# A mixture-of-experts stage on one core: from every expert on every token to visits of 128 scattered rows

## What is computed

```python
h = layernorm(x).reshape(T, d)                 # T = 2048, d = 256
scores = softmax(h @ gate_w.T)                 # 16 experts
topk_w, topk_idx = top_k(scores, 6)
cw = zeros((T, 16)); cw[t, topk_idx[t]] += topk_w[t]
y = 0
for e in range(16):
    g = h @ w_gate[e].T                        # 176 columns
    u = h @ w_up[e].T
    y = y + cw[:, e:e + 1] * (silu(g) * u @ w_down[e].T)
x = x + y
```

## Time and profile before

| | |
|---|---|
| runs, us | 647.69, 657.57, 657.59 (median 657.57) |
| span of the profiled execution, us | 653.6 |
| PE busy | 593.8 us (91%), 3642 matmuls |
| DVE busy | 402.8 us (62%) |
| ACT busy | 295.4 us (45%) |
| POOL busy | 167.2 us (26%) |
| TensorE clock granted, mean | 0.962 |

### The profile page before, as it was taken

How to read it: one execution, slowest core, us unless ns; L and a number is a source line. 1 busy time by engine, 2 the same in 40 slices (tenths; PEclk the granted TensorE clock), 3 DMA queues, 4 the chain that set the end, 5 groups by cost and what they waited for, 6 DMA issues and landing times.

```text
span 653.6 us, 10661 instructions
## 1 busy us (share of the span) xinstructions
PE 593.8 (91%) x3642; PEld 468.5 (72%) x3642; DVE 402.8 (62%) x772; ACT 295.4 (45%) x479; POOL 167.2 (26%) x261
## 2 busy tenths in 40 slices
PE   5889999887888658699999999999999999999995
PEld 4667777663555446588888888888888888888884
DVE  5757877689989635367666555555555555555553
ACT  3585666468879633344444333333333333333331
POOL 6534775938868562000000000000000000000000
PEclk9789999799989857899999999999999999999999
DMA  9700000000000042344543132111231221231211
GB/s 254 254 2 2 1 3 2 1 1 2 1 2 1 1 162 77 87 129 135 141 133 104 59 97 98 65 65 65 64 124 63 64 68 66 82 100 65 64 60 46
DMA packets 37464, 45.90 MB, mean 70 GB/s; under 512 B 10720, under 2 KB 24688, under 8 KB 37296
## 3 DMA queue, kind: packets, MB, share of 16 engines
q1 hardware_dynamic: 34304, 41.19, 20.8%
q0 software_dynamic: 1008, 3.67, 1.7%
q10 hardware_dynamic: 2112, 0.52, 0.4%
HBM read 41.04 MB, written 4.33 MB: 69 GB/s over the span
## 4 chain that ended last, share of the span: by engine, by line
PE 61%; POOL 1%; DVE 1%; ACT 1%; issue 0%; DVEq 0%; POOLq 0%
PE psG L1373 6%; PE psY L1386 6%; PE psG L1375 6%; PE psG L1374 6%; PE psY L1389 6%; PE psU L1375 6%; PE psU L1373 6%; PE psY L1388 6%; PE psU L1374 6%; PE psAux L1314 1%; PE psT L1314 1%; PE psY L1334 1%; PE psT L1399 1%; POOL r_rstd L1280 1%; ACT gw L1500 0%
## 5 line engine op out<-in xcount | busy, mean ns | idle before, releaser
L1472 ACT ACTIVATE act_hi<-x_tok 128x512 fp32r<-128x512 f32 x88 | 55.5, 632 | 161.7 <-DVE x_tok L1601 161.7
L1594 DVE TENSOR_TENSOR x_tok<-psU,x_tok 128x512 f32<-128x512 f32 x88 | 60.8, 691 | 103.3 <-PE psU L1375 103.1
L1605 DVE TENSOR_TENSOR act_lo<-x_tok,act_hi 128x512 fp32r<-128x512 f32 x88 | 60.9, 693 | 62.5 <-ACT act_hi L1472 62.4
L1291 POOL DMA_DIRECT2D out_dram<-x_tok x3 | 2.3, 773 | 300.7 <-DVE x_tok L1612 300.7
L1466 ACT ACTIVATE x_tok<-psG 128x512 f32<-128x512 f32 x88 | 52.7, 600 | 58.4 <-PE psG L1375 58.2
L1386 PE MATMUL psY<-act_hi,wd_lo 128*128 128x512 f32 x176 | 71.1, 404 | 4.9 <-DVE act_lo L1605 4.9
L1373 PE MATMUL psG<-h3T_hi,wg_lo 128*128 (+1 forms) x176 | 69.9, 397 | 0.3 <-DVE logit L1638 0.3
L1389 PE MATMUL psY<-act_hi,wd_hi 128*128 128x512 f32 x176 | 69.2, 393 | 0.0
L1374 PE MATMUL psG<-h3T_lo,wg_hi 128*128 (+1 forms) x176 | 69.1, 392 | 0.0
L1388 PE MATMUL psY<-act_lo,wd_hi 128*128 128x512 f32 x176 | 69.1, 392 | 0.0
L1375 PE MATMUL psG<-h3T_hi,wg_hi 128*128 (+1 forms) x176 | 69.0, 392 | 0.0
(11 more groups left out here) (226 smaller groups left out, 1170.5 us busy)
## 6 DMA issues: line engine op xcount, KB each, us to landing
cw_rows<-cw_spill SPq DMA_DIRECT2D x80, 128.0 KB, 2.9
cw_rows<-cw_spill SPq DMA_DIRECT2D x16, 224.0 KB, 3.0
cw_rows<-cw_spill SPq DMA_DIRECT2D x16, 192.0 KB, 2.7
w_stage<-in_L_ffn_w_gate_dram SPq DMA_DIRECT2D x11, 256.0 KB, 2.8
w_stage<-in_L_ffn_w_up_dram SPq DMA_DIRECT2D x11, 256.0 KB, 2.8
cw_rows<-cw_spill SPq DMA_DIRECT2D x16, 160.0 KB, 2.5
wg_nat<-in_L_attn_w_gate_dram SPq DMA_DIRECT2D x1, 2048.0 KB, 16.4
x_spill<-x_tok SPq DMA_DIRECT2D x1, 2048.0 KB, 7.3
```

The lines of the kernel that those rows point to most:

```text
L1472: nc.scalar.activation(a_hi[s % 2][:, :], a[s % 2][:, :], ACT.Copy).then_inc(s_ahi, 1)
L1594: nc.vector.tensor_tensor(a[s % 2][:, :], psU[s % 2][:, :], a[s % 2][:, :], ALU.mult).then_inc(s_t, 1)
L1605: nc.vector.tensor_tensor(a_lo[s % 2][:, :], a[s % 2][:, :], a_hi[s % 2][:, :].bitcast(F32), ALU.subtract).then_inc(s_alo, 1)
```

## The change

The expert loop is replaced. Tiles 0 and 1 (256 tokens, `DENSE`) still go through all 16 experts: 32 **head visits** of 128 tokens (`HEAD`). The other 1792 tokens are sorted by expert: a rank of each token within each expert is counted with matmuls of 0/1 masks (`ranks`) and DVE sums (`chosen`, `slots`), and POOL writes each token's normalised row, with its shares and its token number (288 floats), to a place in that expert's list in DRAM, by indirect DMA: 14 tiles x 6 choices = 84 `scatter`s. The list lengths give a `table` of which 128 rows of which expert come next; 14 x 6 full tiles and up to 15 more that are part full make `NS` = 99 **list visits**.

A visit holds 128 tokens as the stationary operand and streams the expert's weights: PE turns the rows (2 transposes), makes gate and up together (6 matmuls of 352 columns), turns the activations (2 transposes) and makes the output (5 matmuls of 256 columns). For a list visit SP loads the rows into one of 8 slots (`XRING`), with an address that it reads from the table (`value_load`), PE reads which expert's weights to use, and POOL adds the 128 output rows to their tokens' rows in DRAM by an indirect DMA with accumulation (`add_rows`), in turn to two sums. An add waits until the add before last, to the same sum, has landed; a slot is loaded anew when the add of its former rows has landed. At the end both sums are read back, added and stored.

The expert weights are now transposed in 48 units, 9 in the router front (6 before) and 39 between the head visits; they are staged in two buffers instead of four. POOL makes a few constants in the second round of attention.

```diff
+DENSE = 2
+CAP = T + P
+NS = TOPK * (NT - DENSE) + E - 1
+HEAD = E * DENSE
+NV = HEAD + NS
+XRING = 8
+YRING = 4
+W_RING = 2
+FRONT_UNITS = (1, 1, 1, 1, 1, 1, 1, 2)
...
             @block.sync
+                for e in range(E):
+                    if e >= W_RING:
+                        sp.wait_ge(s_wT, 3 * (e - W_RING + 1))
+                        load_up(sp, k, e)
+                    load_down(sp, k, e)
+                sp.wait_ge(s_table, 1)
+                for e in range(E):
+                    at_row = sp.value_load(tail_of[0:1, e:e + 1], min_val=0, max_val=DUMMY)
+                    sp.dma_start(k.rows_dram[bass.ds(at_row, P), :], k.blank[:, :]).then_inc(s_blank, 16)
+                sp.wait_ge(s_scattered, scattered)
...
+                for j in range(NS):
+                    if j >= XRING:
+                        sp.wait_ge(s_added[j % 2], 16 * ((j - XRING) // 2 + 1))
+                    at_row = sp.value_load(row_of[0:1, j:j + 1], min_val=0, max_val=DUMMY)
+                    sp.dma_start(xs[j % XRING], k.rows_dram[bass.ds(at_row, P), :]).then_inc(s_x[j % XRING], 16)
...
+                for n in pairs:
+                    sp.dma_start(k.x[:, n:n + 2, :], k.acc_v[0][:, n:n + 2, :]).then_inc(s_sums[0], 16)
+                for i, n in enumerate(pairs):
+                    sp.wait_ge(s_final, i + 1)
+                    sp.dma_start(k.out_v[:, n:n + 2, :], k.x[:, n:n + 2, :]).then_inc(k.last_stored, 16)
...
             @block.gpsimd
+                def scatter(n, choice):
+                    pool.indirect_dma_start(k.rows_dram, bass.IndirectOffsetOnAxis(
+                        ap=slot[:, n, choice:choice + 1], axis=0), k.xrow[:, n, :], None).then_inc(s_scattered, 16)
+
+                def add_rows(j):
+                    pool.wait_ge(s_y, j + 1)
+                    need(pool, s_added[j % 2], 16 * (j // 2))
+                    pool.indirect_dma_start(k.acc[j % 2], bass.IndirectOffsetOnAxis(
+                        ap=xs[j % XRING][:, TOKEN:TOKEN + 1].bitcast(U32), axis=0), y[j % YRING], None,
+                        compute_op=ALU.add).then_inc(s_added[j % 2], 16)
...
             @block.tensor
+                for v in range(NV + 2):
+                    j = v - HEAD
+                    if j + 2 >= 0 and j + 2 < NS:
+                        x_turned(j + 2)
+                    if j + 1 >= 0 and j + 1 < NS:
+                        e = pe.value_load(expert_of[0:1, j + 1:j + 2], min_val=0, max_val=E - 1)
+                        at_expert[v + 1] = bass.ds(e * FE, FE), bass.ds(e, 1)
...
+                    if v < NV:
+                        gate_up(v, at_expert[v][0])
+                    if 0 < v <= NV:
+                        a_turned(v - 1)
+                    if v > 1:
+                        down(v - 2, at_expert.pop(v - 2)[1])
+                    for u in head_units(v):
                         unit(u)
+                    if v in (0, 4):
+                        ranks(3 + v // 4)
...
             @block.scalar
+                def y_out(j):
+                    act.wait_ge(s_down, HEAD + j + 1)
+                    if j >= YRING:
+                        act.wait_ge(s_added[j % 2], 16 * ((j - YRING) // 2 + 1))
+                    nc.scalar.activation(y[j % YRING], psY[(j + 1) % 2][:, 0:D], ACT.Copy).then_inc(s_y, 1)
...
+                for v in range(NV + 3):
+                    j = v - HEAD
+                    if 0 <= j - 3 < NS:
+                        y_out(j - 3)
+                    if 0 <= j + 2 < NS:
+                        x_high(j + 2)
+                    if v < NV:
+                        silu(v)
+                    if 0 < v <= NV:
+                        a_high(v - 1)
...
             @block.vector
+                for v in range(NV + 1):
+                    j = v - HEAD
+                    if 0 <= j + 2 < NS:
+                        x_low(j + 2)
+                        share_of(j + 2)
+                    if v < NV:
+                        product(v)
+                    if 0 < v <= NV:
+                        a_low(v - 1)
+                    for u in head_units(v):
                         low_weights(u)
+                    if v == 1:
+                        slots(3)
+                    if v == 2:
+                        chosen(4)
+                    if v == 5:
+                        slots(4)
+                    if v == 8:
+                        table()
```

More of the change, by code:

```diff
@@ L1104, in _, with load_up, load_down @@
                         up(n + 2, 0)
[L1107 to L1134, removed]
+ROW = 288
+SHARES = D
+TOKEN = D + E
+DENSE = 2
+CAP = T + P
+DUMMY = E * CAP
+NS = TOPK * (NT - DENSE) + E - 1
[4 more added lines that the diff above has]
+W_RING = 2
+GROUPS = ((0, 2), (2, 6), (6, 10), (10, 14), (14, NT))
+FRONT_UNITS = (1, 1, 1, 1, 1, 1, 1, 2)
+UNITS = 3 * E
+def load_up(eng, k, e):
+    stage, sem = k.w_stage[e % W_RING], k.w_loaded[e % W_RING]
+    for m in range(2):
+        w = k.expert_w[m]
+        eng.dma_start(stage[:, 0, m, :], w[e, 0:P, :]).then_inc(sem, 16)
+        eng.dma_start(stage[0:FE - P, 1, m, :], w[e, P:FE, :]).then_inc(sem, 16)
+def load_down(eng, k, e):
+    down, sem = k.wd_stage[e % W_RING], k.w_loaded[e % W_RING]
+    wd = k.expert_w[2][e].rearrange("(c p) f -> p c f", p=P)
+    eng.dma_start(down[:, :, 0:FE], wd).then_inc(sem, 16)
+    eng.dma_start(down[:, :, FE:FE + 64], wd[:, :, FE - 64:FE]).then_inc(sem, 16)
+EXPERT_LANDED = 96
 def moe_stage(nc, k):
@@ L1216, in _ @@
             def _(sp):
[L1217 to L1227, removed]
@@ L1317, in shares @@
[L1317 to L1325 removed]
+                    e, m = divmod(u, 3)
@@ L1403, in turn, with ranks @@
-                def turn(g):
-                    for s in range(NCH):
-                        front(g, s)
-                        back(g * NCH + s - 1, (s - 1) % NCH, g)
-                        if s in (1, 2):
-                            transposed(g - 1, s - 1)
+                def ranks(g):
+                    first, end = GROUPS[g]
+                    pe.wait_ge(s_mask, g)
+                    need(pe, s_slot, g - 1)
+                    ps = psP[g]
+                    for q in range(end - first):
+                        nc.tensor.matmul(ps[:, q, :], k.before[:, :], maskb[:, first + q, :], start=True, stop=(q == 0))
+                        for p in range(q):
+                            nc.tensor.matmul(ps[:, q, :], k.onesb[:, :], maskb[:, first + p, :], start=False,
+                                             stop=(p == q - 1))
+                    for p in range(end - first):
+                        last = nc.tensor.matmul(ps[:, 4, :], k.onesb[:, :], maskb[:, first + p, :], start=(p == 0),
+                                                stop=(p == end - first - 1))
+                    last.then_inc(s_rank, 1)
@@ new lines, in three_products, with x_turned @@
+                def three_products(out, hi, lo, w_hi, w_lo, first, end):
+                    nc.tensor.matmul(out, hi, w_lo, start=first, stop=False, skip_group_check=True)
+                    nc.tensor.matmul(out, lo, w_hi, start=False, stop=False, skip_group_check=True)
+                    return nc.tensor.matmul(out, hi, w_hi, start=False, stop=end, skip_group_check=True)
+                def x_turned(j):
+                    pe.wait_ge(s_x[j % XRING], 16 * (j // XRING + 1))
+                    need(pe, s_xlo, j - 1)
+                    for c in range(DC):
+                        last = nc.tensor.transpose(psXs[j % 2][:, c, :], xs[j % XRING][:, c * P:(c + 1) * P],
+                                                   k.ident[:, :])
+                    last.then_inc(s_xT, 1)
@@ L1615, in _ @@
                 nc.vector.memset(score[:, :, E:], -1.0)
+                for n in range(2):
+                    nc.vector.memset(runs[n][:, :, 0:8], 0.0)
+                in_turn(nc.vector.tensor_scalar(base[:, 0, :], k.starts, 1.0, None, ALU.mult))
                 dve.wait_ge(s_gwhi, 1)
```

719 lines of the change are left out of this document (381 added, 338 removed).

## The result

The changed kernel takes 687.6 us (median of 4 runs, 684.25 to 690.97), the kernel before on the same chip 656.2: a ratio of 1.056, 95% interval 1.0484 to 1.0636. On another chip it was 688.95 against 653.71, 1.058. It is slower, as forecast, by more than the forecast's 3%. The ratios leave out one run of a slow state further down, 1650.4 us with ten slots, 2.5 times as long as the nine others of that kernel.

What follows compares the result with a forecast made beforehand. The prediction took PE alone to bound the expert loop. Its stages ran to 287 (front), 372 (head), 637 (list visits), 652 (drain) and 672 (tail); with 4 for the median of runs, 676 us, range 628 to 740.

Steps and rivals of the forecast that it cites:

- the scatters are hidden: POOL's 84 scatters, 1.2 us each from about 265, would end at 366, hidden behind the head visits.
- The front: Router front, from 235: would take 52 us, 33 before, and end at 287.
- The head: Head visits, from 287: DVE leads, 85 us to the first list rows at 372.
- rival B: POOL makes descriptors slowly: above 1.27 us a scatter rows are late, 8.4 us per 0.1; at 1.6, 716. Chance 0.18.
- A list visit: List stage: 2.7 us a visit, 98 visits 265 us, until 637; PE waits some 0.7 of each for rows.
- The fixed part of the round trip: List visits: a slot's way to its next use, without four PE visits, 10.8 us, covered by four visit times.
- Drain and tail: After the list visits: drain of 15 us until 652, then reading back, adding and storing the sums until 672.
- The adds alone: List visits: the adds, two under way, would by themselves allow 2.1 us a visit.
- rival A: List visits: adds and loads return fast, add 2.7 instead of 4.2, 2.2 us a visit, 626, 5% faster. Chance 0.30.
- What would show it: List stage signs: PE waits ending at x_tok landings, PE near 75% busy, visits 2.7 apart, adds landing in 3.3.
- C: TensorE's clock: gaps in each visit keep PE at 1.2 GHz, 4.0 us a visit, near 800. Chance 0.05.

Runs made afterwards that it cites:

- the experiment: Changed kernel, with PE reading a visit's table word ahead of its wait for rows instead of behind it: 668.7 us, ratio 1.023 to the kernel before.
- early slots and three sums: Changed kernel, with a slot free once its rows are turned and shares and token numbers copied out, and adds going to three sums: 628.5 us, ratio 0.963.

## Why the prediction was right

The verdict and the mechanism of the list visits held, and one condition, that the scatters are hidden, did not; 676 was 12 us too low. By its steps, against the profiled span of 689.2 (the sum had 672):

- **The front ended some 12 us earlier than said**, near 275 instead of 287: PE's first product of the head stands at 272.1, DVE's at 277.1. The counted links of small DVE operations lay more beside other work than in the sum: DVE is busy 31.5 of 42 us there, and was 16.8 of 37, so it has 14.7 us more work in a front that grew by some 7.
- **The head was right, its cover was not.** The head's visits end at 364, some 89 us later where I had 85. But the scatters, "hidden behind the head", were not: one every 1.31 us on average (1.26 in most) instead of 1.2, 371.9 for the last start instead of an end at 366. The rows below are the last scatter, the first load and the first turn in the changed kernel:

```profile
371.88 0.96 POOL L1306 DMA_INDIRECT rows_by_expert<-x_tok,slot  x1 [0.30 <-issue]
375.07 2.59 SPq L1282 DMA_DIRECT2D x_tok<-rows_by_expert  x3
...
377.06 0.69 PE L1419 MATMUL psX<-ident,x_tok 128*128 128x128 f32 x2 [12.45 <-DMA x_tok<-rows_by_expert]
```

PE waits 12.45 us. The head lost its cover because the front was shorter than said, so rival B came true in place though not in price: its threshold of 1.27 us a scatter, set for a head that ends later, was passed by 0.04, where its price was for 1.6. Landing and first load (377.06 - 372.84 = 4.2 us) were in no term. By luck the errors cancel to 5 us in the start of the list visits, 377 for 372.
- **A list visit, 2.81 for 2.7**, is the largest miss, 10 us over the 98. The fixed part of the round trip was 11.2 instead of 10.8. Its terms: an add 3.8 in the median from start to landing, with SP awake 0.02 later, instead of 4.2; read and load of SP 0.7 + 2.4 instead of 3.5; PE from the turn to the end of the output 2.9 to 3.0 instead of 2.4 and 0.16, with the table read at 0.65 behind a stall (0.7 by the experiment) instead of 0.6; ACT's copy and POOL's start 0.39 + 0.27 instead of 0.38 and 0.2. With the load's median that makes 10.6; landings of 4.2 to 4.5 and loads of 2.8 to 3.7, which the chain has too, can make up the rest. So the add's landing was taken too long, and PE's part and the loads', when SP is late, too short: part of the closeness is errors that cancel. What makes those loads longer stays open.
- **Drain and tail, 16.4 and 20.5, for 15 and 20**, from the last turn at 652.3 to the last add's landing at 668.7 and on to 689.2.
- **The adds alone "would allow 2.1" was wrong**, though it didn't decide here. Two adds in turn took 4.58 and 4.60 us a pair in the chain shown and 4.78 on average with 10 slots, 2.4 each: 3.8 to 4.2 to the landing and 0.7 until POOL starts, where the term of 4.2 was meant to hold both. So below 2.4 a visit the adds bind, and the prediction's rival A, at 2.2, needed them quicker than they are. Its time came out in another kernel by coincidence (626 forecast, 628.5 with early slots and three sums): the adds land no sooner there (4.1 us), and fewer of them are waited for.
- **What would show it** did: PE's waits end at landings into x_tok, visits 2.8 apart, PE busy 84% (75% said; by its pace alone, 2.07 of 2.81, it is 74%), an add 3.8 from issue to landing (3.3 said). C fell: the granted clock of the list visits is 0.95, near the upper level. With 6 slots, where PE waits up to 10 us for rows, it is 0.72, between the two levels.

Three slips in the prediction's working did not decide: twice 0.81 is 1.6, not 1.8 (the upper bound of the add), 3.5 MB at 7.3 us for 2 MB are 12.8 us, not 12, and rival B's scatters at 1.6 would by its own threshold be 28 us late, not 31.

On the two figures that the prediction took from the Trainium skill: an add of 128 KB landed 3.8 us after its issue. The Trainium skill (DMA: Bandwidth & Descriptors, Anatomy of one DMA) would have given 2.3, an estimate from its formula, which prices no accumulation; the trace does not agree for this kind, and the 3.3 from the rows came nearer. The table reads took 0.27 us on SP and 0.30 on PE, with 0.15 of register work behind. The Trainium skill (same page, Latency and other measured facts) has a floor of about 600 ns for a tensor_load; this trace is below it.

## What to carry to other kernels

When a dense loop becomes visits that pass through memory, cost the ring before the arithmetic: write down every step between the reuse of a buffer, add it up, divide by the visits that the buffers cover beyond the busy engine's own, and do the same for each other ring (here the sums and the output tiles), since removing one stall only uncovers the next: alone, freeing the slots gave 31 us and four sums cost 24; together, with three sums, they gave 59. A buffer should be held no longer than its data are read, so copy out the few words that a late step needs. And a register read behind a wait was paid in full here, 0.65 us; in front of the wait or behind queued work it cost nothing.

## What the runs showed of the hardware

An indirect DMA with accumulation occupies POOL for 1.56 us for 128 rows of 1 KB, without accumulation 0.96, and between two adds or two scatters at least 0.30 us pass. The DMA engines pay too: for the same bytes, the queue of POOL's transfers took (packets, MB, share of 16 engines) in the changed kernel and with plain stores:

```profile
q0 software_dynamic: 18288, 25.37, 21.0%
```

```profile
q0 software_dynamic: 8784, 25.37, 10.2%
```

The difference is 9504 packets, 96 for each add, and half of the engines' time on this queue. The landing of an add also releases the two queues unlike: SP went on after 0.02 us, and POOL's sequencer after 0.03, but POOL's next add began 0.69 later still (the chain with 10 slots).
